# Eight-head expert lookup after attention: gathered expert numbers summed by TensorE, and half of the scatter products in the second half of a turn

## The reference, cut to what matters

```
q = (xn @ w_q.T).reshape(b, t, H, 2, DK)             # H = 8 heads, two halves
sim1, sim2 = products of q's halves with keys         # 32 keys for each half
s1, i1 = top_k(sim1, 8);  s2, i2 = top_k(sim2, 8)
all_idx = i1[..., :, None] * 32 + i2[..., None, :]    # expert numbers 0..1023
all_sc  = s1[..., :, None] + s2[..., None, :]
fs, pk  = top_k(all_sc, 8)
fi      = take_along_axis(all_idx, pk)                # 64 expert numbers a token
hidden  = gelu(xn . expert_down[fi]) * relu(fs)
out     = sum over the 64 of hidden * expert_up[fi]
```

## Time and profile before

| | us |
|---|---|
| timed, median of 3 runs | 1803.34 (1799.84 to 1803.65) |
| profiled execution, its own time | 1807.29 |
| span of the profiled execution | 1805.4 |
| busy: DVE, PE, ACT, POOL | 1553.2, 1316.3, 891.4, 743.6 |

### The profile page before, as it was taken

One profiled execution on the slowest core, in us unless ns is written; L12 is line 12 of the kernel. 1 busy time (PEld: TensorE's weight loads), 2 busy tenths in 40 slices (PEclk: granted clock), 3 DMA queues, 4 the chain that ended last, 5 costly groups with the idle time before them and its releaser, 6 DMA issues. The chain is left out here.

```text
span 1805.4 us, 53473 instructions
## 1 busy us (share of the span) xinstructions
PE 1316.3 (73%) x19456; PEld 930.9 (52%) x19632; DVE 1553.2 (86%) x7082; ACT 891.4 (49%) x1518; POOL 743.6 (41%) x1088
## 2 busy tenths in 40 slices
PE   3556678776868878676877868687776778777646
PEld 2333365554546555454646545464655546455436
DVE  2137998989899898989989898998989899898995
ACT  1656555636454553645455464545546454553110
POOL 1226353544445254444525344452534446242330
PEclk7688789897987969788897868879787877968666
DMA  2000000000000000000000000000000000000000
GB/s 76 1 7 7 6 9 7 14 8 8 8 7 15 7 14 8 13 3 7 15 7 15 7 13 2 7 15 7 14 7 13 8 1 15 1 14 2 8 1 15
DMA packets 29974, 18.58 MB, mean 10 GB/s; under 512 B 1824, under 2 KB 29216, under 8 KB 29728
## 3 DMA queue, kind: packets, MB, share of 16 engines
q1 hardware_dynamic: 29728, 15.23, 3.0%
HBM read 11.04 MB, written 4.19 MB: 8 GB/s over the span
## 5 line engine op out<-in xcount | busy, mean ns | idle before, releaser
L579 ACT ACTIVATE prob<-S 128x512 f32<-128x512 f32 x640 | 368.3, 599 | 393.0 <-PE S L749 223.4
L841 PE MATMUL G<-whot,onehot 128*128 128x16 bf16 x12288 | 382.9, 173 | 91.4 <-DVE hid L1238 71.1
L841 PEld LDWEIGHTS G<-whot,onehot 128*128 128x128 bf16 x12288 | 372.0, 102 | 130.3 <-DVE hid L1238 66.2
L1200 DVE TENSOR_TENSOR onehot<-lo_no,esel 128x1024 bf16<-128x1024 uint16 x512 | 380.4, 797 | 0.1
L416 POOL TENSOR_TENSOR qk_a<-qk_n,cosw 128x256 f32<-128x256 f32 x64 | 58.0, 906 | 489.2 <-DVE qk_n L1017 453.0
L749 PE MATMUL S<-causal,ident_b 128*128 128x128 bf16 x1024 | 218.8, 245 | 38.6 <-issue 19.1
L699 PE MATMUL S<-ident_b,stack 128*128 128x128 bf16 x1024 | 100.4, 271 | 155.2 <-POOL stack L432 122.0
L462 POOL TENSOR_TENSOR gat<-gat,cande 128x1280 f16<-128x1280 f16 x64 | 151.4, 2366 | 135.9 <-DVE gat L1161 135.9
L699 PEld LDWEIGHTS S<-ident_b,stack 128*128 128x128 bf16 x1024 | 84.3, 124 | 194.1 <-POOL stack L432 146.5
L1141 DVE FIND_INDEX8 topi<-topv,sims 128x8 uint16<-128x32 f32 x1024 | 166.2, 185 | 0.0
L747 PE MATMUL S<-qT,kT_even 128*128 128x384 bf16 (+3 forms) x440 | 127.8, 323 | 39.8 <-ACT prob L579 39.5
(11 more groups left out here) (139 smaller groups left out, 2543.9 us busy)
## 6 DMA issues: line engine op xcount, KB each, us to landing
xa<-in_L_attn_x SPq DMA_DIRECT2D x16, 256.0 KB, 2.8
xr<-in_L_attn_x SPq DMA_DIRECT2D x16, 256.0 KB, 3.0
out<-r SPq DMA_DIRECT2D x16, 256.0 KB, 2.5
onehot<-in_L_ffn_expert_down SPq DMA_DIRECT2D x1, 512.0 KB, 6.0
up<-in_L_ffn_expert_up SPq DMA_DIRECT2D x1, 512.0 KB, 7.0
onehot<-in_L_ffn_keys SPq DMA_DIRECT2D x1, 256.0 KB, 6.5
onehot<-in_L_attn_w_qkv SPq DMA_DIRECT2D x1, 192.0 KB, 4.8
onehot<-in_L_attn_w_proj SPq DMA_DIRECT2D x1, 64.0 KB, 4.8
```

The source lines that it names most:

```text
L579: act.activation(dst, src, ACT.Exp, scale=SCALE).then_inc(exp_done.sem, 1)
L841: last = nc.tensor.matmul(bank[:, 16 * i:16 * i + 16], onehot[:, pair, t, :], whot[:, t, w_part, :], start=(w_part == 0), stop=(w_part == 2))
L1200: dve.tensor_tensor(onehot[:, pair, t:t + 8, :].rearrange("p t (c i) -> p t c i", i=2), lo, e, ALU.is_equal)
```

## The change

The expert numbers are no longer summed by POOL and DVE. `gather` keeps its product and loses its addition; `selected` and the tile `esel` go. The tile `gat` has its places (`NCAND`, 20) outermost, and PE sums over them: `turn_numbers` runs 20 products of 64 columns of `gat` with the identity for each tile, accumulated in PSUM, which also turns the numbers over. They run at steps 12, 19, 26 and 31. `transpose_selection` at step 34 transposes the scores alone.

On VectorE `weighted_one_hots` 0 and 1 move from the end of the turn into the row of one-hots (after the 8th, and after the 16th one), and `apply_weights` 2 and 3 move from the next turn's first part to the end of this one. On PE parts 8 to 15 of the scatter products move with them, so that 16 parts run in the second part of the turn and 16 in the 40 steps. `WEIGHT_STEPS` becomes steps 7 to 14 and 17 to 24.

```diff
-        gat_done = signal("gat_done", 2 * NT)
-        esel_done = signal("esel_done", NT)
+        gat_done = signal("gat_done", NT)
+        numbers_turned = signal("numbers_turned", NT)
...
+        NUMBER_STEPS = [12, 19, 26, 31]
         SELECTION_STEP = 34
-        WEIGHT_STEPS = list(range(1, 9)) + list(range(13, 29))
+        WEIGHT_STEPS = list(range(7, 15)) + list(range(17, 25))
...
-                pool.wait_ge(gat_done.sem, gat_done.value(b, 2 * t + 1))
-                pool.tensor_tensor(g[:, :, 0:10], g[:, :, 0:10], g[:, :, 10:20], ALU.add)\
...
+            def turn_numbers(b, t):
+
+                rows = slice(t % 2 * 64, t % 2 * 64 + 64)
+                pe.wait_ge(gat_done.sem, gat_done.value(b, t + 1))
+                if t == 0:
+                    wait_f_empty(pe, b, "sel")
+                for c in range(NCAND):
+                    last = nc.tensor.matmul(bank_f("sel")[rows, t // 2 * P:(t // 2 + 1) * P], gat[:, t % 2, c].rearrange("p h k -> p (h k)"),
+                                            ident_b[:, :], start=(c == 0), stop=(c == NCAND - 1),
+                                            skip_group_check=True)
+                last.then_inc(numbers_turned.sem, 1)
...
-                        weights(older, 8 + WEIGHT_STEPS.index(step))
+                        weights(older, 16 + WEIGHT_STEPS.index(step))
...
+                    if late is not None and step in NUMBER_STEPS:
+                        turn_numbers(late, NUMBER_STEPS.index(step))
...
+                if late is not None:
+                    for part in range(0, 8):
+                        weights(late, part)
                 if nxt is not None:
                     transpose_stack(nxt, 2)
                 if late is not None:
-                    for part in range(0, 4):
+                    for part in range(8, 12):
                         weights(late, part)
                 if nxt is not None:
                     transpose_stack(nxt, 3)
                 if late is not None:
-                    for part in range(4, 8):
+                    for part in range(12, 16):
                         weights(late, part)
...
                     weighted_one_hots(older, 2)
-                    apply_weights(older, 2)
                 if late is not None:
                     top_pairs(late, 0)
                     top_keys(late, 2)
                 if older is not None:
-                    apply_weights(older, 3)
                     weighted_one_hots(older, 3)
                 if late is not None:
                     top_pairs(late, 1)
-                    selected(late, 0)
                     top_keys(late, 3)
-                if b is not None:
-                    normalise_o(b, 0)
                 if older is not None:
                     apply_weights(older, 4)
+                if b is not None:
+                    normalise_o(b, 0)
...
-                one_hots(hot(5, 9))
+                one_hots(hot(5, 8))
+                if late is not None:
+                    weighted_one_hots(late, 0)
...
                     one_hots(hot(14, 16))
+                if late is not None:
+                    weighted_one_hots(late, 1)
                 one_hots(hot(16, 18))
...
-                one_hots(hot(20, 32))
-                if late is not None:
-                    weighted_one_hots(late, 0)
-                    weighted_one_hots(late, 1)
+                one_hots(hot(20, 28))
+                if late is not None:
+                    apply_weights(late, 0)
+                one_hots(hot(28, 30))
+                if late is not None:
+                    apply_weights(late, 1)
                 if b is not None:
                     top_keys(b, 0)
                 if late is not None:
-                    apply_weights(late, 0)
+                    apply_weights(late, 2)
+                one_hots(hot(30, 32))
                 if b is not None:
                     top_keys(b, 1)
                 if late is not None:
-                    apply_weights(late, 1)
+                    apply_weights(late, 3)
```

## The result

The changed kernel takes 1926.49 us (median of 4 runs, 1924.77 to 1933.63) against 1803.49: 1.0695 times the kernel before, with a 95% interval of 1.0664 to 1.0725. Its profiled execution has a span of 1923.6 us and took 1925.4. The forecast of slower was right, the size was not: +123 us where +77 was foretold, and 1.5 us above 1925, the upper end of the range. Every later run has its own executions of the kernel before beside it (medians 1798.84 to 1805.34 us), and its ratio is against those.

The account below looks back on a forecast made before the run. A loop through DVE and PE bounds the kernel, neither engine alone: 40.0 + 24.6 + 22.7 + 23.5 = 110.8 us a turn against 104.95, +77 us in total, 1880 us; own range 1850 to 1910, whole range 1815 to 1925.

Parts of the forecast that it names:

- two roads: After the second `normalise`: one through (b) and (c); one through POOL's `split`, stack transposes and first scores, shorter by 2.25 us.
- (a): `decode` to the end of the second `normalise`: 34.9 us, plus 5.1 for two `weighted_one_hots`, becomes 40.0 us.
- (b): End of the second `normalise` to the end of DVE's turn: 27.6 us becomes 24.6, with a new wait of about 2.
- rival 1: Milder loop: PE at full clock, DVE's new wait in (b) not showing; 107.6 us a turn, 1835 us; chance 0.17.
- (c): DVE in the 40 steps, up to the end of `apply_weights` 4: 25.6 us less 2.9 that leave, 22.7 us.
- (d): PE from its release by `apply_weights` 4 through step 34 to the next `decode`: 16.8 us becomes 23.5.
- Rival 2: Dear number products, 0.11 us each: the 60 cost 3.3 us more, 114.1 a turn, 1926 us; chance 0.11.
- The turn before 282: One turn ahead of the 13 measured, also with attention and scatter products: counted as 5.85 us longer, like them.
- The last turn: Final turn, with no attention on PE: DVE's four `selected` come off, 5 us gained.
- the tail: Work behind the last turn: ends within 1 us of today's, since chunks 4 to 7 still must be made and applied.

Follow-up runs that it names:

- n_only: Kernel before with TensorE summing the numbers (number products at steps 14, 22, 28, 31) and no scatter work moved: 1817.35 us, ratio 1.0071.
- w_apply45: w_only with `apply_weights` 4 ahead of `selected` 0 and `top_keys` 3, and `apply_weights` 5 ahead of `top_pairs` 2: 1798.22 us, ratio 0.9985.
- a_ahead: a_best1 with both `weighted_one_hots` where the change put them, ahead of the second `normalise`: 1801.03 us, ratio 1.0002.
- a_sims: Changed kernel with the similarities of tile 3 computed beside those of tile 2 at step 4, not step 14: 1901.01 us, ratio 1.0533.
- a_two: Changed kernel with 18 of the 20 number products of each tile left out (expert numbers wrong): 1872.81 us, ratio 1.0404.
- a_apply4: Changed kernel with `apply_weights` 4 ahead of `top_keys` 3 on VectorE: 1826.61 us, ratio 1.0134.
- b_apply45: Kernel before with `apply_weights` 4 ahead of `selected` 0 and `top_keys` 3, and `apply_weights` 5 ahead of `top_pairs` 2: 1778.77 us, ratio 0.9874.
- a_best1: Changed kernel with both `weighted_one_hots` back behind the second `normalise`, `apply_weights` 4 and 5 moved ahead, scatter and number steps retuned: 1778.12 us, ratio 0.9860.
- a_best2: a_best1 with the number products of tiles 0 and 1 at steps 15 and 22 instead of 13 and 21: 1772.47 us, ratio 0.9850.
- b_apply4: Kernel before with `apply_weights` 4 ahead of `selected` 0 and `top_keys` 3: 1810.22 us, ratio 1.0052.
- w_only: Kernel before with the scatter work moved alone, POOL and VectorE still summing the numbers: 1910.19 us, ratio 1.0585.

## Why the prediction was right in its sign and wrong in its size

**The bound.** That a loop through both engines sets the time, and DVE's busy share does not, holds: n_only takes work off DVE and gets slower, w_apply45 only reorders and gains 112 us. Which of its two roads closes the loop differs: through `apply_weights` in the kernel before and in the changed one, through the first scores in n_only and a_ahead.

**(a), foretold 40.0, measured 40.9.** The mechanism was right, the size short. The two calls cost (timeline of DVE, start of each and of what follows):

```profile
1095.96 0.68 DVE L1229 TENSOR_TENSOR hot_hi<-hi_no,ehi 128x1024 bf16<-128x1024 uint16 x1
...
1098.49 0.25 DVE L1072 RECIPROCAL rden<-A 128x16 f32<-128x16 f32 x1
...
1115.90 0.69 DVE L1229 TENSOR_TENSOR hot_hi<-hi_no,ehi 128x1024 bf16<-128x1024 uint16 x1
...
1119.38 1.28 DVE L1211 TENSOR_TENSOR onehot<-lo_no,elo 128x1024 bf16<-128x1024 uint16 x2
```

2.53 us where POOL is idle, as priced from the earlier trace rows, and 3.48 where POOL's `split` runs beside it. I took the lower bound for both; the second belonged near the upper one. That is 0.9 us a turn.

**(b), foretold 24.6, measured 24.25.** Right but for 0.35 us, with the wait before `apply_weights` 2 (1.6 us, 13 times; foretold about 2). The stack transposes again took half-speed time, 16 in 1.68 us (1141.17 to 1142.85, granted clock 0.50):

```profile
1141.17 1.89 PE L700 MATMUL S<-ident_b,stack 128*128 128x128 bf16 x16 [4.39 <-POOL stack L432]
1142.85 2.75 PE L851 MATMUL G<-whot,onehot 128*128 128x16 bf16 x96
```

The scatter products in the hole before them were free, as foretold. Full clock there, which rival 1 wanted, did not come.

**(c), foretold 22.7, measured 24.7.** This is the step that failed. I took (c) as DVE's own work and subtracted what leaves it. I looked for PE's arrival only at step 17, and not for what PE gives to DVE on the way: step 14 carries the similarities that `top_keys` 3 needs. Before, they came 17.5 us after the first scores (means of 13 turns), and DVE never waited for them. Now they come at 19.4 us, since PE waits for `weighted_one_hots` 2 at step 7 and runs 20 number products at step 12, while DVE enters the 40 steps 2.4 us after the first scores in place of 4.6 and is there before them. The 21.6 us of waits for ACT are 1.7 us a turn; a_sims removes them and gets 22.97. The other 0.3 us is a reading: 25.6 was one turn's (c), the mean of before is 25.9, and 25.9 less the 2.9 that leave is 23.0. I also called PE's wait at step 17 no longer than the old one; at 5.1 us it is 1.4 times the mean of before (47.6 / 13 = 3.7). PE arrives there 22 us after the first scores, as foretold, but the release comes at 27.1 and not at 24.3, 2.0 us of it by (c), the rest because the first scores come 21.9 us after `normalise` and not 23.0.

**(d), foretold 23.5, measured 23.7.** Right. The number products cost 1.23 us a group at full clock, against 1.1 reckoned from the earlier trace rows, and up to 2.3 for the one group behind the wait; without 18 in 20 of them (d) is 2.3 us shorter, and the forecast had 2.4 for its three groups. The 14.5 us that the forecast gives (d) at full clock stood on no row. Rival 2 doubled the price of all products, and its 1926 us is the measured time. That is luck: a_two shows 3.75 us a turn for 72 products, not 6.3.

**The sum.** The four misses make 113.6 - 110.8 = 2.8 us a turn, 36 us over 13 turns. The turn before 282 became 8.5 us longer instead of 5.85, and the first `decode` comes 2.7 us later (183.98 against 181.31), which I had put at nothing. The last turn gained 4.9 us (84.2 against 89.1), and the tail moved by 0.5, both as foretold. 36 + 3 + 3 on the foretold 77 is 119, and the spans differ by 118. The medians differ by 123, since the profiled execution of before lies 4 us above its median and that of the changed kernel 1 us below.

**The parts of the change.** Against the kernel before of the same runs, n_only costs 12 us and the moved scatter work alone 105. The 12 us are not the price of the products alone, as its first scores come later by 2.0 us a turn, which the changed kernel doesn't show (21.9 us after `normalise`). Nearly all of the 105 us was the order of `apply_weights` 4 and 5 on DVE, which the new steps made critical: w_apply45 gives 112 us back, a_apply4 gives 100 back in the changed kernel, and a_ahead, with both chunks ahead and the scatter steps retuned, the rest to 1801. But the same reordering helps the kernel before as well, and that is the kernel to compare with. b_apply45, without anything of the change, has a ratio of 0.9874 (0.9823 to 0.9926); the change at its best has 0.9860 (a_best1) and 0.9850 (a_best2), inside that interval. No gain of the change itself is shown.

**The two lengths of a turn.** The turns of the changed kernel are of two kinds, nine of 112.3 to 113.6 us and four of 115.1 to 115.7. PE's own rows tell what differs between steps 7 and 12. The same 122 matmuls, in the turn from 743.18 (115.5 us) and in that from 974.40 (113.0 us):

```profile
814.16:821.96 7.80, 7.80 (x122) 4.18 (x119) 7.46 (x67) 1.20 (x2) 3.67 (x3) 0.57 0.01 3
1045.37:1050.75 5.38, 5.38 (x122) 3.42 (x119) 5.16 (x53) 1.19 (x2) 2.62 (x1) 1.00 0.02 3
```

The granted clock is 0.57 in one and 1.00 in the other, so a part of the first stretch runs at 1.2 GHz and all of the second at 2.4 GHz. Taken over 5.2 us from 70.8 us after `decode`, six of the 13 turns have a clock of 1.00 and waits of DVE for the similarities of 0.8 us, three have 0.67 or 0.68 and 1.7 to 1.8 us, three have 0.51 to 0.57 and 3.2 to 3.3 us, and the last has 0.50 and 2.0. With 0.8 us in all of them, (c) would be 0.9 us shorter, some 12 us in 13 turns (an estimate from these waits). So of the 1.7 us missed in (c) about half is the ring itself and half the clock ahead of step 14.

**What stays open.** Why the clock is lower there in some turns and not in others: no run varied it alone. What PE waits for ahead of the first scores in n_only. And no run separated the retuned steps of a_ahead from its `apply_weights` 5.

## What to carry to other kernels

Where two engines hand work to each other several times a turn, write down for each piece not only who waits for it but what the waiting engine will have handed over by then; here the ring without slack showed as a wait of the same length in turn after turn (5.13, 5.12, 5.13 us). An operation that another engine waits for belongs ahead of everything in its own queue that it doesn't depend on, and it is of no use to bring one forward if the next hand-over stays where it was: b_apply4 lost 0.5%, b_apply45 gained 1.3%. Prices of edits that share a wait neither add nor subtract (w_only was missed by 42 us that way). And when a reordering rescues a change, try it on the kernel without the change too: here it was worth as much there.

## What the runs showed of the hardware

Twenty accumulating products of 64 stationary and 128 moving columns, fp16 with bf16, take 1.23 us at a granted clock of 1.00, 0.062 us each, and 1.5 to 2.3 us behind an idle time of 5.1 us. A stationary half as wide was not cheaper than the 0.055 us of the earlier trace rows. POOL's product of `gather` takes 2.61 us in the new layout against 2.37, for the same 1280 elements. It is the layout and not what runs beside it: n_only, with the new layout and the old places of the work, has 2.61, and w_only, the other way round, 2.37. In the changed kernel (page):

```profile
L465 POOL TENSOR_TENSOR gat<-gat,cande 128x1280 f16<-128x1280 f16 x64 | 167.0, 2610 | 184.6 <-DVE gat L1178 184.6
```
